# First stage of a graph-attention and expert kernel: four buffers a hand-over, longer lags, and one half of a quarter's encoding ahead of the softmax's exponential

## Chip, cores, metric

One core of one Trainium2 chip. The metric is the device time of one execution in microseconds (us), the median of several.

## What is computed

```python
x = x + elu(attention @ Wh)        # a graph-attention layer on layernorm(x)
x = x + expert_ffn(layernorm(x))   # then a feed-forward layer, one expert a row
# x: 8192 x 256 f32, adj: 8192 x 8192 int32, ones at a rate of 0.000488
def gnn(h, adj, W, a):
    Wh = h @ W                                     # 256 x 256
    e = (Wh @ a1)[:, None] + (Wh @ a2)[None, :]
    e = where(e > 0, e, 0.2 * e)
    e = where(adj > 0, e, -9e15)
    return elu(softmax(e, axis=1) @ Wh)
def ffn(x, router_w, router_b, W1, b1, W2, b2):    # 32 experts, hidden size 64
    idx = argmax(x @ router_w.T + router_b)
    return relu(relu(x @ W1[idx] + b1[idx]) @ W2[idx] + b2[idx])
```

## The kernel before

The 8192 rows are 64 strips of 128. The work has three stages, and each engine runs an order written out by hand, with semaphores between the engines.

**First stage** (8 groups of 8 strips; functions `group` and `prepare`). Each strip s goes through a line of engines: VectorE normalises it (`normalise`, L985, into `xn`), GpSimd adds it to a running sum (`row_sum`, L583), TensorE transposes it (L1485), ScalarE copies the transpose out of PSUM (L709, into `xT`), TensorE multiplies it with the weights (L1494, into `psW`), VectorE copies the 258 columns to the table rows (`table_rows`, L993). `xn`, `xT`, the PSUM tiles of the transposes and `psW` have two buffers each. TensorE's order is T(s), W(s-1), where T is the pair of transposes and W the product; VectorE's is N(s), C(s-2), where N is the normalising and C the copy. Both empty the line at a group's end. In the second half of a group VectorE also takes the statistics of the next group (L967, two strips a step) and at its end the variances (L973, L975); GpSimd then takes the power -1/2 of all eight (`inverse_stds`, L569), without which the next group's N(0) can't start. After the group's last C, GpSimd writes the eight table rows to HBM (L593). One buffer of the means (`mv`) and of the inverse deviations (`rs`) serves all groups.

Beside this, each group handles one half strip of `adj`: SyncE loads it (L427, 2 MB, three buffers), ScalarE turns the int32 entries into two sets of fp8 signs (`signs`: L717 the even bytes, L719 the odd ones, a quarter strip at a time, two quarters a group, after strips 2 and 6), TensorE folds them at the group's end (`fold`, L1512 and L1514, into `psF`), and VectorE takes the largest words (`search`, L891), right after the next group's N(0). After every second group VectorE decodes the columns found (L897 to L957), spread over the even groups.

At the end of the stage the mean row goes through TensorE and VectorE and is written to HBM (L598); when all writes have landed, GpSimd starts the first gathers (L611).

**Second stage**: 64 rounds u, one strip each, four strips ahead in `adj`. GpSimd gathers the table rows of the columns found (L611) and scatters finished rows to their expert's region (L633); VectorE computes scores and softmax, decodes, places; ScalarE encodes four quarters of `adj` a round (`signs`, eight instructions of L717 and L719) and takes the softmax's exponential (`softmax_exp`, L749), which waits for the row maximum of VectorE (`nmx`, L1106). SyncE issues the load of a half strip when ScalarE has finished the half that lay in its buffer.

**Third stage**: the experts' blocks, unchanged.

Of the kernel before, what the change touches and what calls it, by code (L numbers as in the profile page):

```python
# [5 lines left out]
P = 128  # L6
D = 256
DH = D // P
# [12 lines left out]
THIRDS = 3  # L21
FOLD = 8
PAIRS = FOLD // 2
GROUP = 8
# [12 lines left out]
def gat_moe(nc, x, adj, gW, ga, rw, rb, W1, b1, W2, b2, out, table, region):  # L37
# [23 lines left out]
    with ctx:  # L61
# [106 lines left out]
        diag = sb("diag", [P, 8, P])  # L168
# [64 lines left out]
        psXn = [psT, psO[0]]  # L233
# [286 lines left out]
        def _(pool):  # L520
# [44 lines left out]
            def inverse_stds(g):  # L565

                pool.wait_ge(v_var, g + 1)
                pool.nop(nofuse=True)
                pool.tensor_tensor(rs[:, :], ve[:, :], minus_half[:, :], ALU.pow).then_inc(pl_rs, 1)  # L569
# [7 lines left out]
            def row_sum(s, r):  # L577
# [5 lines left out]
                pool.tensor_tensor(xn_sum[:, :], xn_sum[:, :], xn[r % 2][:, :], ALU.add).then_inc(pl_sum, 1)  # L583

            def group(g, par, i, behind, ahead):
                for r in range(GROUP):
                    row_sum(g * GROUP + r, r)
                if ahead:
                    inverse_stds(g + 1)
# [101 lines left out]
        def _(act):  # L691
# [12 lines left out]
            def transposes(s, r):  # L704

                act.wait_ge(pe_xT, s + 1 + 2)
                act.wait_ge(pe_wh, s + 1)
                act.nop(nofuse=True)
                act.activation(xT[r % 2][:, :, :].rearrange("p h n -> p (h n)"), psXn[r % 2][:, 0:D], ACT.Copy).then_inc(a_xT, 1)  # L709

            def signs(t, par, q, strip):
# [5 lines left out]
                act.activation(sign_of[par][q][0], raw_of[b][q % 2][0], ACT.Identity, bias=minus_tiny[:, 0:1], scale=TINY,  # L717
                               saturate=False)
                act.activation(sign_of[par][q][1], raw_of[b][q % 2][1], ACT.Sign, bias=minus_half[:, 0:1],  # L719
                               saturate=False).then_inc(a_sg, 1)  # L720
# [45 lines left out]
            def step(u, par, do, strip):  # L766
# [8 lines left out]
                if do.ahead:  # L775
                    signs(u + LAG + 1, 1 - par, 1, strip)
# [954 lines left out]
```

## Time and profile before

| | us |
|---|---|
| median of 3 runs (1185.07 to 1197.87) | 1185.52 |
| profiled execution | 1188.4 |
| its span, first to last instruction | 1186.6 |
| first stage, first N to last C | 24.2 to 147.7 |
| second stage, first to last exponential | 176.3 to 1006.8 |

The profiled execution has 1.8 us outside its span, and is 2.9 us above the median.

### The profile page before, as it was taken

How to read it: one execution, taken by the hardware profiler on the slowest of the kernel's cores; microseconds unless marked ns; L12 is line 12 of the kernel's file. 1: busy time of each engine (PE TensorE's matmuls, PEld its weight loads, DVE VectorE, ACT ScalarE, POOL GpSimd, SP SyncE). 2: the span in 40 equal slices, each digit the busy share in tenths (PEclk: the TensorE clock that was granted, in tenths of full speed). 3: DMA queues.
4: the chain of work that ended last, by engine and by line, in shares of the span. 5: the costliest groups of instructions: out<-in, count | busy, mean ns of one | idle time of the engine just before them, and what ended most of it. 6: DMA issues, size and time to landing. Idle time of an engine off the chain costs nothing.

```text
span 1186.6 us, 25008 instructions
## 1 busy us (share of the span) xinstructions
PE 900.9 (76%) x4388; PEld 560.6 (47%) x4389; DVE 894.5 (75%) x4327; ACT 795.4 (67%) x1339; POOL 656.9 (55%) x700
## 2 busy tenths in 40 slices
PE   2777728788878888688887878878888875558995
PEld 1545515444444444354454444445445444446774
DVE  5788727688888878788888878878888876555563
ACT  0444549688887878688788877878878831136663
POOL 3555545556656655555565556655566556326664
PEclk9999959899999989899999999989999986679998
DMA  6677788899999999899999989998999995035651
GB/s 227 219 270 266 295 335 345 318 376 377 376 371 368 362 349 365 330 341 381 363 381 349 368 323 371 366 361 336 374 381 383 341 251 129 29 105 162 173 170 60
DMA packets 84715, 357.33 MB, mean 301 GB/s; under 512 B 26006, under 2 KB 52591, under 8 KB 68289
## 3 DMA queue, kind: packets, MB, share of 16 engines
q1 hardware_dynamic: 56226, 296.78, 67.7%
q0 software_dynamic: 27712, 60.06, 14.7%
q8 instruction: 12, 0.20, 0.1%
q14 instruction: 29, 0.24, 0.1%
q10 hardware_dynamic: 736, 0.05, 0.0%
HBM read 343.67 MB, written 32.05 MB: 317 GB/s over the span
## 4 chain that ended last, share of the span: by engine, by line
DVE 29%; DMA 23%; issue 22%; PE 13%; POOL 7%; DVEq 2%; ACT 2%; POOLq 0%; ACTq 0%
DMA regions<-x,posu 13%; DMA G_all<-wh_table,idx 7%; POOL G_all L611 4%; PE psO L1704 2%; DVE top_word L891 2%; PE psW L1494 2%; PE psO L1577 2%; POOL out_x L673 2%; DVE xn L1158 1%; DVE begun L1058 1%; DVE lidx L1173 1%; PE psO L1503 1%; DVE oh L1181 1%; DVE xn L985 1%; DVE el L1132 1%
## 5 line engine op out<-in xcount | busy, mean ns | idle before, releaser
L611 POOL DMA_INDIRECT G_all<-wh_table,idx x384 | 398.7, 1038 | 136.4 <-issue 128.7
L717 ACT ACTIVATE sg<-raw_all,minus_tiny 128x1024 fp8e4<-128x1024 int32 x256 | 311.8, 1218 | 0.1
L719 ACT ACTIVATE sg<-raw_all,minus_half 128x1024 fp8e4<-128x1024 int32 x256 | 311.1, 1215 | 0.0
L1503 PE MATMUL psO<-word_no,share 128*128 128x512 bf16 x885 | 244.0, 411 | 0.0
L633 POOL DMA_INDIRECT regions<-x,posu x64 | 67.4, 1053 | 213.9 <-DVE idx L1050 115.7
L1577 PE MATMUL psO<-G_all,diag 128*128 128x256 f32 x640 | 163.2, 405 | 22.9 <-DVE diag L1115 22.9
L1577 PEld LDWEIGHTS psO<-G_all,diag 128*128 128x128 f32 x640 | 124.3, 201 | 64.9 <-issue 48.4
L1512 PE MATMUL psF<-sg,fold_w 128*128 128x512 bf16 x512 | 136.0, 389 | 7.3 <-DVE top_word L891 2.7
L1503 PEld LDWEIGHTS psO<-word_no,share 128*128 128x128 bf16 x885 | 93.6, 111 | 92.9 <-issue 26.8
L749 ACT ACTIVATE pr<-ee,nmx 128x16 f32<-128x16 f32 x64 | 19.7, 307 | 146.3 <-DVE nmx L1106 146.3
L673 POOL DMA_INDIRECT out_x<-raw_all,tok x81 | 78.9, 974 | 56.6 <-issue 29.9
L891 DVE MAX8 top_word<-psF 128x8 f32<-128x256 f32 x256 | 103.0, 425 | 6.7 <-PE psF L1514 0.5
L1494 PE MATMUL psW<-w_aug,xT 128*128 128x258 f32 x256 | 69.5, 395 | 13.8 <-ACT xT L709 13.8
L583 POOL TENSOR_TENSOR xn_sum<-xn_sum,xn 128x256 f32<-128x256 f32 x64 | 47.5, 742 | 40.7 <-DVE xn L985 39.8
L1512 PEld LDWEIGHTS psF<-sg,fold_w 128*128 128x128 bf16 x512 | 47.1, 108 | 43.8 <-issue 13.4
L1704 PE MATMUL psO<-x_sb,hT 128*128 x162 | 56.0, 428 | 8.9 <-ACT hT L825 3.7
L1563 PE MATMUL psW<-slot_s,to_row 128*128 128x11 f32 x128 | 22.3, 248 | 49.3 <-DVE slot_s L1086 49.1
L627 POOL TENSOR_TENSOR x<-ve,minus_half 128x1 f32<-128x1 f32 x64 | 36.8, 576 | 35.6 <-DVE x L1154 34.7
L1563 PEld LDWEIGHTS psW<-slot_s,to_row 128*128 128x128 f32 x128 | 22.8, 204 | 69.8 <-issue 68.7
L1494 PEld LDWEIGHTS psW<-w_aug,xT 128*128 128x128 f32 x256 | 44.8, 195 | 22.7 <-issue 18.9
L817 ACT ACTIVATE w_b<-x_sb 128x129 f32 x84 | 26.3, 313 | 43.0 <-ACT hT L825 30.2
L1086 DVE TENSOR_SCALAR slot_s<-slot_col,G_all 128x11 f32<-128x11 f32 x64 | 16.6, 260 | 47.9 <-DMA G_all<-wh_table,idx 46.9
(217 smaller groups left out, 1837.5 us busy)
## 6 DMA issues: line engine op xcount, KB each, us to landing
raw_all<-in_adj SPq DMA_DIRECT2D x128, 2048.0 KB, 10.0
raw_all<-regions SPq DMA_DIRECT2D x84, 130.0 KB, 2.2
wh_table<-G_all POOLq DMA_DIRECT2D x8, 1040.0 KB, 10.0
x_sb<-in_x SPq DMA_DIRECT2D x8, 1024.0 KB, 5.7
G_all<-wh_table,idx POOLq DMA_INDIRECT x384, 6.1
regions<-pad_row SPq DMA_DIRECT2D x32, 130.0 KB
x_sb<-in_L_ffn_W SPq DMA_DIRECT2D x4, 512.0 KB
x_sb<-in_L_ffn_W SPq DMA_DIRECT2D x8, 256.0 KB
```

The costliest lines, as they stand in the source:

```text
L583: pool.tensor_tensor(xn_sum[:, :], xn_sum[:, :], xn[r % 2][:, :], ALU.add).then_inc(pl_sum, 1)
L611: pool.indirect_dma_start(out=G[par][:, k, :], out_offset=None, in_=table[:, :], in_offset=bass.IndirectOffsetOnAxis(ap=idx[par][:, k:k + ...
L633: pool.indirect_dma_start(out=region[:, :], out_offset=bass.IndirectOffsetOnAxis(ap=posu[par][:, 0:1], axis=0), in_=x1[par][:, :], in_offs ...
L673: pool.indirect_dma_start(out=out[:, :], out_offset=bass.IndirectOffsetOnAxis(ap=tok[r % STORES][:, 0:1], axis=0), in_=yb[r % STORES][:, : ...
L717: act.activation(sign_of[par][q][0], raw_of[b][q % 2][0], ACT.Identity, bias=minus_tiny[:, 0:1], scale=TINY, saturate=False)
L719: act.activation(sign_of[par][q][1], raw_of[b][q % 2][1], ACT.Sign, bias=minus_half[:, 0:1], saturate=False).then_inc(a_sg, 1)
L891: v.max(top_word[:, q, :], psF[q // 2][:, q % 2 * WORDS:(q % 2 + 1) * WORDS]).then_inc(v_top, 1)
L1494: mm = pe.matmul(psW[r % 2][:, 0:D + 2], xT[r % 2][:, h, :], w_aug[:, h, :], start=(h == 0), stop=(h == DH - 1))
L1503: pe.matmul(psO[par][:, :], share[:, :], word_no[:, 0:2, :].rearrange("p q w -> p (q w)"), start=True, stop=True)
L1512: pe.matmul(words, fold_w[:, j, :], sg[par][:, 2 * h:2 * h + 2, j * WORDS:(j + 1) * WORDS], start=(j == 0), stop=False)
L1577: pe.matmul(psO[par][:, 0:D], diag[:, k, :], G[par][:, k, 0:D], start=(k == 0), stop=False)
L1704: pe.matmul(psO[r % 2][:, 0:D], hT[r % 2][:, :], w2_sb[:, bass.ds(e, 1), :].rearrange("p o n -> p (o n)"), start=True, stop=True).then_inc ...
```

## The change

In the first stage `xn` and `xT` get four buffers (the two new ones lie in `diag`, which is free until the second stage), the transposes' PSUM tiles three, `mv` and `rs` two. TensorE's order becomes T(s), W(s-2) and VectorE's N(s), C(s-3), across the groups' borders; only the last group empties the line. The next group's statistics move to strips 2 to 5, the variances behind strip 5, the power behind the sixth row sum. A group's table write moves behind the third row sum of the next group. ScalarE encodes one instruction after every second strip rather than two after every fourth. SyncE issues a group's x and `adj` loads when two strips of the group two before are normalised, six strips earlier. The fold stays at the group's end in TensorE's order, then behind T(7) and W(5). In the second stage the even bytes of the third quarter are encoded ahead of the exponential; the odd ones stay behind `elu_exp`.

```diff
+COPY_LAG = 3
...
-        mv = sb("mv", [P, GROUP, 2])
+        mv = [sb(f"mv{i}", [P, GROUP, 2]) for i in range(2)]
-        rs = sb("rs", [P, GROUP])
-        xn = [sb(f"xn{i}", [P, D]) for i in range(2)]
-        xT = [sb(f"xT{i}", [P, DH, P]) for i in range(2)]
+        rs = [sb(f"rs{i}", [P, GROUP]) for i in range(2)]
+        diag = sb("diag", [P, 8, P])
+        xn = [sb(f"xn{i}", [P, D]) for i in range(2)] + [diag[:, 2 * i:2 * i + 2, :].rearrange("p h n -> p (h n)") for i in range(2)]
+        xT = [sb(f"xT{i}", [P, DH, P]) for i in range(2)] + [diag[:, 4 + 2 * i:6 + 2 * i, :] for i in range(2)]
...
-        psXn = [psT, psO[0]]
+        psXn = [psT, psO[0], psO[1]]
...
@@ load_group (SyncE)
-                sp.wait_ge(v_xn, g * GROUP + GROUP)
+                sp.wait_ge(v_xn, g * GROUP + 2)
@@ group (GpSimd)
+            def group(g, par, i, behind, ahead):
+                for r in range(GROUP):
+                    row_sum(g * GROUP + r, r)
+                    if behind and r == COPY_LAG - 1:
+                        write_rows(g - 1, 1 - par)
+                    if ahead and r == 5:
+                        inverse_stds(g + 1)
             groups(pool, group)
+            write_rows(NG - 1, (NG - 1) % 2)
@@ transposes, group (ScalarE)
-                act.wait_ge(pe_wh, s + 1)
+                if s >= 4:
+                    act.wait_ge(pe_wh, s - 1)
...
-                    if r % 4 == 2:
-                        signs(i, i % 2, 2 * par + r // 4, divmod(i, THIRDS))
+                    if r % 2 == 0:
+                        signs(i, i % 2, 2 * par + r // 4, divmod(i, THIRDS), range(r // 2 % 2, r // 2 % 2 + 1))
@@ step (ScalarE)
                 if do.ahead:
                     signs(u + LAG + 1, 1 - par, 1, strip)
+                    signs(u + LAG + 1, 1 - par, 2, strip, range(1))
                 if do.attend:
                     softmax_exp(u)
                 if do.post:
                     elu_exp(u - 1)
                 if do.ahead:
-                    signs(u + LAG + 1, 1 - par, 2, strip)
+                    signs(u + LAG + 1, 1 - par, 2, strip, range(1, 2))
                     signs(u + LAG + 1, 1 - par, 3, strip)
@@ normalise, prepare (VectorE)
-                v.wait_ge(pe_xT, s + 1)
-                if s >= 2:
-                    v.wait_ge(pl_sum, s - 1)
+                if s >= 4:
+                    v.wait_ge(pe_xT, s - 1)
+                    v.wait_ge(pl_sum, s - 3)
...
-                    if r >= 2:
-                        table_rows(g, par, i, r - 2)
-                    if ahead and r >= GROUP // 2:
+                    if g * GROUP + r >= COPY_LAG:
+                        table_rows(g * GROUP + r - COPY_LAG)
+                    if ahead and 2 <= r < 6:
                         for k in range(2):
-                            group_stats(g + 1, 1 - par, next_i, (r - GROUP // 2) * 2 + k)
-                if ahead:
-                    group_variances(g + 1)
-                table_rows(g, par, i, GROUP - 2)
-                table_rows(g, par, i, GROUP - 1)
+                            group_stats(g + 1, 1 - par, next_i, (r - 2) * 2 + k)
+                    if ahead and r == 5:
+                        group_variances(g + 1)
@@ transposes, group (TensorE)
-                pe.wait_ge(a_xT, s + 1)
+                if s >= 3:
+                    pe.wait_ge(a_xT, s)
...
                     transposes(g * GROUP + r, r)
-                    if r:
-                        table_rows(g * GROUP + r - 1, r - 1)
-                table_rows(g * GROUP + GROUP - 1, GROUP - 1)
+                    if g * GROUP + r >= 2:
+                        table_rows(g * GROUP + r - 2, r)
                 fold(i, i % 2, par)
```

## Rows read from the trace of the kernel before

**Rows 1.** The page, busy tenths in 40 slices of the span.
```profile
DVE  5788727688888878788888878878888876555563
DMA  6677788899999999899999989998999995035651
```
**Rows 2.** Windows of the first stage: the stage, an even group, an odd group.
```profile
24.20:147.30 123.10, 92.39 (x421) 61.48 (x422) 92.82 (x317) 60.56 (x104) 66.20 (x79) 1.00 0.71 252
86.98:102.80 15.82, 11.47 (x54) 7.42 (x53) 13.96 (x54) 7.27 (x12) 8.52 (x10) 1.00 0.76 267
102.80:117.74 14.94, 11.26 (x54) 7.49 (x53) 11.07 (x39) 7.21 (x12) 8.56 (x10) 1.00 0.80 279
```
**Rows 3.** Timeline (start, duration, engine), end of an even group, start of the next.
```profile
96.93 0.39 DVE L985 TENSOR_SCALAR xn<-x_sb,mv,rs 128x256 f32<-128x256 f32 x1
...
97.47 0.41 PE L1485 MATMUL psT<-ident,xn 128*128 128x128 f32 x2 [0.94 <-DVE xn L985]
...
97.71 1.04 PE L1494 MATMUL psW<-w_aug,xT 128*128 128x258 f32 x4
...
100.73 0.42 DVE L993 COPY G_all<-psW 128x258 f32<-128x258 f32 x1
100.97 1.65 POOL L569 TENSOR_TENSOR rs<-ve,minus_half 128x8 f32<-128x8 f32 x1 [1.44 <-DVE ve L975]
...
101.03 1.11 PE L1494 MATMUL psW<-w_aug,xT 128*128 128x258 f32 x4 [0.98 <-ACT xT L709]
...
101.98 1.02 PE L1512 MATMUL psF<-sg,fold_w 128*128 128x512 bf16 x4
...
102.84 0.38 PE L1514 MATMUL psF<-word_no,share 128*128 128x512 bf16 x1
...
103.36 0.76 DVE L891 MAX8 top_word<-psF 128x8 f32<-128x256 f32 x2 [0.15 <-PE psF L1514]
```
**Rows 4.** Timeline, two VectorE instructions that meet a row sum, first stage.
```profile
91.65 0.82 DVE L932 SCALAR_TENSOR_TENSOR key<-bits,code 128x128 f32<-128x128 int32 x1
...
105.12 0.90 DVE L985 TENSOR_SCALAR xn<-x_sb,mv,rs 128x256 f32<-128x256 f32 x1 [0.69 <-POOL xn_sum L583]
```
**Rows 5.** Timeline of the first group: two copies and the variances.
```profile
31.64 0.43 DVE L993 COPY G_all<-psW 128x258 f32<-128x258 f32 x1 [1.40 <-PE psW L1494]
...
32.89 0.43 DVE L993 COPY G_all<-psW 128x258 f32<-128x258 f32 x1 [0.50 <-PE psW L1494]
...
38.93 0.17 DVE L975 TENSOR_SCALAR ve<-mv 128x8 f32<-128x8 f32 x1
```
**Rows 6.** Timeline, the last V, the stage's last copy, the mean's write, the first gather.
```profile
131.51 0.42 DVE L993 COPY G_all<-psW 128x258 f32<-128x258 f32 x1
...
147.26 0.43 DVE L993 COPY G_all<-psW 128x258 f32<-128x258 f32 x1 [1.86 <-PE psW L1494]
...
151.07 0.55 POOL L598 DMA_DIRECT2D wh_table<-mean_sb  x1 [1.91 <-DVE mean_sb L1044]
...
163.03 1.14 POOL L611 DMA_INDIRECT G_all<-wh_table,idx  x1 [11.41 <-issue]
```
**Rows 7.** Waits from 300 to 900 us: total, times, longest.
```profile
ACT pr L749 <- DVE nmx L1106: 91.2, 44, 6.5
...
DVE slot_s L1086 <- DMA G_all<-wh_table,idx: 18.6, 8, 4.6
DVE x L1140 <- DMA regions<-x,posu: 17.4, 20, 1.6
```
**Rows 8.** Timeline of ScalarE, the exponential of one round.
```profile
604.44 0.31 ACT L749 ACTIVATE pr<-ee,nmx 128x16 f32<-128x16 f32 x1 [1.98 <-DVE nmx L1106]
```
**Rows 9.** One line of the source, L427: the adjacency loads.
```profile
DMA to landing us min/median/max: 7.3/10.0/11.8
```
**Rows 10.** Timeline, the power and a VectorE instruction at once, second stage.
```profile
597.01 0.59 POOL L627 TENSOR_TENSOR x<-ve,minus_half 128x1 f32<-128x1 f32 x1
597.02 0.28 DVE L1058 TENSOR_SCALAR begun<-slot_no,tail_row 128x128 f32<-128x128 f32 x1
```

More of the change, by code:

```diff
@@ L568, in inverse_stds @@
                 pool.nop(nofuse=True)
[L569 removed]
+                pool.tensor_tensor(rs[g % 2][:, :], ve[:, :], minus_half[:, :], ALU.pow).then_inc(pl_rs, 1)
             inverse_stds(0)
@@ L582, in row_sum, with write_rows @@
                 pool.nop(nofuse=True)
[L583 to L587, printed above, removed]
-                if ahead:
-                    inverse_stds(g + 1)
+                pool.tensor_tensor(xn_sum[:, :], xn_sum[:, :], xn[r % 4][:, :], ALU.add).then_inc(pl_sum, 1)
+            def write_rows(g, par):
                 pool.wait_ge(v_wh, g * GROUP + GROUP + 2)
@@ L706, in transposes, with signs @@
                 act.wait_ge(pe_xT, s + 1 + 2)
-                act.wait_ge(pe_wh, s + 1)
+                if s >= 4:
+                    act.wait_ge(pe_wh, s - 1)
                 act.nop(nofuse=True)
-                act.activation(xT[r % 2][:, :, :].rearrange("p h n -> p (h n)"), psXn[r % 2][:, 0:D], ACT.Copy).then_inc(a_xT, 1)
-            def signs(t, par, q, strip):
+                act.activation(xT[s % 4][:, :, :].rearrange("p h n -> p (h n)"), psXn[s % 3][:, 0:D], ACT.Copy).then_inc(a_xT, 1)
+            def signs(t, par, q, strip, bytes=range(2)):
                 b, count = half_place(strip, q // 2)
@@ L716, in signs @@
                 act.nop(nofuse=True)
[L717 to L720, printed above, removed]
+                if 0 in bytes:
+                    act.activation(sign_of[par][q][0], raw_of[b][q % 2][0], ACT.Identity, bias=minus_tiny[:, 0:1], scale=TINY,
+                                   saturate=False)
+                if 1 in bytes:
+                    act.activation(sign_of[par][q][1], raw_of[b][q % 2][1], ACT.Sign, bias=minus_half[:, 0:1],
+                                   saturate=False).then_inc(a_sg, 1)
             def group(g, par, i, behind, ahead):
@@ L972, in group_variances @@
                 for r in range(GROUP):
-                    v.bn_aggr(mv[:, r, :], st[:, r, :]).then_inc(v_st, 1)
+                    v.bn_aggr(mv[g % 2][:, r, :], st[:, r, :]).then_inc(v_st, 1)
                 v.wait_ge(v_st, g * 2 * GROUP + 2 * GROUP)
-                v.tensor_scalar(ve[:, :], mv[:, :, 1], EPS, None, ALU.add).then_inc(v_var, 1)
+                v.tensor_scalar(ve[:, :], mv[g % 2][:, :, 1], EPS, None, ALU.add).then_inc(v_var, 1)
             def normalise(g, par, r):
@@ L981, in normalise, with table_rows @@
                     v.wait_ge(pl_rs, g + 1)
-                v.wait_ge(pe_xT, s + 1)
-                if s >= 2:
-                    v.wait_ge(pl_sum, s - 1)
-                v.tensor_scalar(xn[r % 2][:, :], x_rows(s), mv[:, r, 0:1], rs[:, r:r + 1],
+                if s >= 4:
+                    v.wait_ge(pe_xT, s - 1)
+                    v.wait_ge(pl_sum, s - 3)
+                v.tensor_scalar(xn[s % 4][:, :], x_rows(s), mv[par][:, r, 0:1], rs[par][:, r:r + 1],
                                 ALU.subtract, ALU.mult).then_inc(v_xn, 1)
-            def table_rows(g, par, i, r):
-                v.wait_ge(pe_wh, g * GROUP + r + 1 + 2)
+            def table_rows(s):
+                g, r = divmod(s, GROUP)
+                i, par = divmod(g, 2)
+                v.wait_ge(pe_wh, s + 1 + 2)
                 if r == 0:
@@ L1039, in _ @@
             groups(v, prepare)
+            for s in range(NS - COPY_LAG, NS):
+                table_rows(s)
             v.wait_ge(pe_sum, 1)
@@ L1481, in transposes @@
                 pe.wait_ge(v_xn, s + 1 + 2 * GROUP)
-                pe.wait_ge(a_xT, s + 1)
+                if s >= 3:
+                    pe.wait_ge(a_xT, s)
                 pe.nop(nofuse=True)
                 for h in range(DH):
-                    mm = pe.transpose(psXn[r % 2][:, h * P:(h + 1) * P], xn[r % 2][:, h * P:(h + 1) * P], ident[:, :])
+                    mm = pe.transpose(psXn[s % 3][:, h * P:(h + 1) * P], xn[s % 4][:, h * P:(h + 1) * P], ident[:, :])
                 mm.then_inc(pe_xT, 1)
@@ L1493, in table_rows @@
                 for h in range(DH):
-                    mm = pe.matmul(psW[r % 2][:, 0:D + 2], xT[r % 2][:, h, :], w_aug[:, h, :],
+                    mm = pe.matmul(psW[s % 2][:, 0:D + 2], xT[s % 4][:, h, :], w_aug[:, h, :],
                                    start=(h == 0), stop=(h == DH - 1))
@@ L1524, in _ @@
             groups(pe, group)
+            for s in range(NS - 2, NS):
+                table_rows(s, s)
             pe.wait_ge(pl_sum, NS)
```

9 lines of the change are left out of this document (4 added, 5 removed).

## The prediction

> **What bounds the kernel now.** I read the page's slices first [rows 1]: up to slice 5 (148 us) both VectorE and the DMA engines have gaps, then the DMA engines stand at 9 tenths nearly everywhere and VectorE at 7 or 8. So the two halves of the change fall on stages with different limits. The windows of the first stage [rows 2] say that no engine fills it: in 123.1 us VectorE is busy 92.8, TensorE 92.4, GpSimd 66.2, ScalarE 60.6. An even group, which also decodes, takes 15.82 us with VectorE busy 13.96; an odd one 14.94 with 11.07. VectorE's idle time is thus 1.86 and 3.87 us a group. It is the engine nearest to its bound, and in even groups there is little left.
>
> The timeline at a group's end [rows 3] shows where that idle time is. Let V be the moment after the variances, 100.73. The power runs from 100.97 to 102.62; TensorE's last product starts at 101.03, the fold at 101.98, its last matmul at 102.84, and the search starts at 103.36, V+2.63. Between V and there VectorE does two copies, two small ones and N(0), about 1.4 us, and idles 1.2.
>
> **First stage, the group's end.** The change runs the power under N(6), C(3), N(7), C(4), and so seems to take the wait away. But the fold stays behind T(7) and W(5) in TensorE's order, and N(6) and N(7) now come after the variances. I walk it with the steps of [rows 3]:
> - N(6) starts at V. A transpose starts 0.54 after its N (96.93 to 97.47), the product 0.24 later (97.71): T(6) at V+0.54, W(4) at V+0.78.
> - What follows a product starts 0.95 after it (101.03 to 101.98): T(7) at V+1.7, W(5) at V+1.95, the fold at V+2.9.
> - The fold's last matmul comes 0.86 after its first (101.98 to 102.84), the search 0.52 after that (to 103.36): V+4.3.
>
> Within these 4.3 us VectorE has N(6), C(3), N(7), C(4), N(0): with 0.40 and 0.43 each, less some overlap, 1.7 us. It idles 2.6 us, not 1.2. The power ends at V+1.9 and is hidden; the fold is what is late next.
>
> **First stage, the rest of a group.** Elsewhere an odd group idles 3.87 - 1.2 = 2.7 us now. The longer lags take most of it: W(s-2) finds its xT finished, and N(s) needs no sum of two strips ago. What stays is C(7) behind W(7) behind T(1) behind the late N(1), some 0.9 us by the same steps (N(1) follows the search; 0.54 + 0.24 + 1.1 for T and W, less N(2) in between). An N that meets a row sum under way takes 0.90 rather than 0.40 [rows 4]; an odd group has two such, 0.9 us together. With the table write in mid-group, not ahead of the sums, GpSimd isn't behind there, and these 0.9 us go. Odd group: 11.07 - 0.9 + 2.6 + 0.8 = 13.6, against 14.94: 1.3 to 1.4 us better. Even group: it idles 1.86 - 1.2 = 0.66 elsewhere, which goes, and two N give back 0.6; the `key` instruction that runs into a row sum, 0.82 [rows 4], stays, since it follows N as before. 13.96 - 0.6 + 2.6 = 16.0, against 15.82: 0.2 worse. Odd groups 1, 3, 5: -4.1; even groups 2, 4, 6: +0.5.
>
> **First group.** Its statistics move into waits for the slow first products. Now C(1) starts at 31.64 and C(2) at 32.89 [rows 5], and the variances at 38.93. After: C(1) at 31.6, a pair of statistics and N(5) beside W(2), C(2) at about 33.0, two more statistics (0.7), the variances (0.75): V at 34.5 rather than 39.0. This is -4.4.
>
> **Last group.** No statistics, and the line empties in the order T(7), W(5), fold, W(6), W(7). With 1.1 us a product the last copy starts some 17.3 us after the last V; now it is 15.8 (131.51 to 147.26, [rows 6]): +1.5. The mean's write at 151.07 waits for TensorE's last sum, which now stands behind the fold, and after behind W(7): only +0.5 to +0.8 there. The first gather, 163.03, waits for that write's landing and the last table write's, which come within 1 us of each other: +0.7.
>
> **The other edits** of this stage I cost at nothing. The loads issued six strips earlier use DMA engines that idle between 24 and 37 us [rows 1]; SyncE's queue keeps its order and its wait for ScalarE. The table write queues behind the third row sum and waits for C(7) at most 1 us; behind it stand row sums 3 and on, four strips ahead of their reader. If one write landed 4 us late, C(0) of the group after the next would wait for it. Encoding in single instructions halves the time that an xT can stand behind them.
>
> Sum of the first stage: -4.4 - 4.1 + 0.5 + 0.7 = -7.3 us. The second stage starts at a landing, not at a clock, so all of it is passed on.
>
> **Second stage.** ScalarE waits for `nmx` 91.2 us in 44 rounds, 2.07 a round [rows 7], at [rows 8] 1.98. One encoding instruction (1.2 us, 1.1 from start to start) fits in; and of the waits that I saw hardly one is under 1.1 (the shortest 1.04), so the exponential is not late. It finishes its quarter 1.1 us earlier, and so does the release of the buffer. But ScalarE then waits for the next keys; VectorE sees nothing. What VectorE waits for here is DMA: 18.6 us for gathers in 8 rounds and 17.4 for scatters in 20 [rows 7]. The moved instruction needs the half strip's second half 1.1 us earlier after a release that is 13 us old, and the loads land in at most 11.8 [rows 9]: a bound of nothing above, one late load below. Every second load is issued 1.1 us earlier, and they lie more evenly (by the ends of ScalarE's second and fourth quarters 5.7 and 7.5 us apart now, 6.8 and 6.4 after), which may spare or add DMA waits: no row shows this, so I bound it by the row of the scatters, half of 17.4 either way, and take 0, as the engines are at 9 tenths already.
>
> **Sum.** The profiled execution 1188.4 (span 1186.6 plus 1.8) less 7.3 is 1181.1; it stands 2.9 above the median, so the forecast on the median's scale is 1185.5 - 7.3 = 1178.2.
>
> **A rule against it.** A row sum in progress stretches N to 0.90 [rows 4]. A power does not: `begun`, a tensor_scalar of 128x128 that starts 0.01 us after it, takes 0.28 [rows 10], less than an undisturbed N of twice the columns. The Trainium skill (SBUF — State Buffer, SBUF: two separate sides) says that VectorE in a two-port mode and GpSimd take a shared pair of ports by an exclusive lock for the whole instruction, and the loser blocks; by that, N(7) would wait for the power's end. The row of the sums agrees with it, the row of the power doesn't.
>
> **Rivals.**
> - *The power of eight columns blocks N(7) after all* (it is 1.65 us long in the first stage, 0.59 in [rows 10]). N(7) would end at V+2.05, T(7) start at V+2.2, and the search at V+4.75: 0.5 more in seven groups, 3.5. Then 1185.5 - 3.8 = 1182. Against it: [rows 10]. 0.13.
> - *The fold is not late*, and VectorE runs at its own work: odd groups 10.2 + 1.2 = 11.4, even ones 13.4 + 0.5 = 13.9, so 3 x 3.5 + 3 x 1.9 + 4.4 - 0.7 = 19.9: 1166; or the fold is late, and the evener loads spare half the scatter waits: 1178 - 9 = 1169. For it: the idle time is there; against it, the order of TensorE's queue. 0.22 together.
> - *Slower: earlier releases bunch the loads onto the gathers.* The place is VectorE's wait for the gather of the slots (`slot_s`, now 18.6 us in 8 rounds, the longest 4.6, [rows 7]). With three more of the longest it is -7.3 + 13.8 = +6.5, 1192; it decides from two on, and passes 1% at five. For it: DMA at 9 tenths; against: two loads a round remain, with evener distances. 0.10.
> - *The gain is not passed on*: the adjacency stream, not the start, sets the second stage's end, and the stage takes back what it started early: 1185. For it: DMA at 9 tenths; against: ScalarE's releases, not bytes, pace the loads. 0.12.
> - The forecast itself: 0.43, its own range 1174 to 1182.
>
> **How the numbers follow.** A measurement here tells about 1% (12 us) from no change. The range reaches from the second rival's 1166, a little further for both its parts together, to the slow rival's near side: 1164 to 1190. Faster by over 1%, below 1173.7: all of the second rival and a fifth of the forecast, 0.31. Slower by over 1%, above 1197.4: the far half of the slow rival, 0.05. The rest is 0.64.
>
> **What would show it.** In the profile after: V of the first group at 34.5; odd groups 13.6 and even ones 16.0 from search to search; VectorE idle ahead of the search on the fold (now 0.15, after about 1.4); no wait of N for a row sum in odd groups; the last C at about 140; first gather near 156; exponentials after a wait of 0.3 to 0.9 and the same distances of 12.4 and 13.4. I am wrong if the odd and even groups lose more than 1.5 us each, if the power stretches N(7), or if the second stage's length of 830 us between first and last exponential changes by more than 8.

## The result, and the profile after

The changed kernel takes 1209.93 us (median of 4 runs, 1205.33 to 1211.92) against 1185.39 for the kernel before on the same chip: ratio 1.0233, 95% interval 1.0175 to 1.0291. It is slower by about 25 us where I had forecast 7 us faster. Its profiled execution took 1210.87 us, with a span of 1209.1.

**Where the time went.** Two moments split the profiled executions: the last C of the first stage and the softmax's exponentials (first and last).

| us | before | after |
|---|---|---|
| start of the last C | 147.3 | 146.9 |
| first exponential | 176.3 | 177.5 |
| first to last exponential | 841.2 | 862.4 |

(The 830 us that the prediction gives for the last row, and the 1006.8 in the table of the profile before, leave out the 64th exponential, 10.7 us after the 63rd.) So the first stage gained nothing, and the second lost 21 us. The page's slices, to be read beside [rows 1]:

```profile
DVE  5877627888878888888887888878887876555563
DMA  7668769999999999999998999989998996135552
```

They show nearly nothing: 2.5% of a stage spread over 63 rounds doesn't reach a tenth of a slice. The waits from 300 to 900 us do show it (engine, line, releaser: us in total, times, longest), against [rows 7]:

```profile
DVE slot_s L1099 <- DMA G_all<-wh_table,idx: 49.4, 22, 5.7
...
DVE x L1153 <- DMA regions<-x,posu: 0.6, 2, 0.3
```

VectorE's wait for a gather went from 18.6 us in 8 rounds to 49.4 in 22, which is every second round of this window. The wait for a scatter went from 17.4 to 0.6, presumably because a scatter has landed by the time that a late round asks for it; no run isolates that. Net, 14 us in 600, hence some 20 over the stage.

**What a late round looks like.** Timeline after: the last gather of a round, the load issued ahead of it on SyncE's queue (SPq), and the reader of the gathers.

```profile
602.12 0.33 SPq L428 DMA_DIRECT2D raw_all<-in_adj  x1
...
602.25 1.01 POOL L617 DMA_INDIRECT G_all<-wh_table,idx  x1 [0.30 <-DVE x L1167]
...
609.35 0.23 DVE L1099 TENSOR_SCALAR slot_s<-slot_col,G_all 128x11 f32<-128x11 f32 x1 [1.88 <-DMA G_all<-wh_table,idx]
```

The same three in a round of the kernel before:

```profile
595.98 1.01 POOL L611 DMA_INDIRECT G_all<-wh_table,idx  x1 [0.30 <-issue]
596.96 0.33 SPq L427 DMA_DIRECT2D raw_all<-in_adj  x1
...
601.53 0.30 DVE L1086 TENSOR_SCALAR slot_s<-slot_col,G_all 128x11 f32<-128x11 f32 x1
```

Before, the load of 2 MB goes out 0.98 us behind the last gather, and the reader comes 5.55 us after the gather without a wait. After, the load is 0.13 us ahead of it, and the gather's data is there only 7.1 us after its issue, 1.88 later than VectorE wanted it. Between 420 and 620 us after, all seven late rounds have the load 0.11 to 0.14 us ahead and a wait of 1.81 to 2.24; in the rounds between them the load is 0.9 to 2.6 behind, and there is no wait. From 300 to 900 us it is 21 of 21 rounds with the load ahead that wait, and none of 18 with it 0.9 us or more behind. ScalarE's exponentials show both kinds of round:

```profile
585.06 0.31 ACT L758 ACTIVATE pr<-ee,nmx 128x16 f32<-128x16 f32 x1 [2.66 <-DVE nmx L1119]
...
597.31 0.31 ACT L758 ACTIVATE pr<-ee,nmx 128x16 f32<-128x16 f32 x1 [0.26 <-DVE nmx L1119]
...
612.24 0.31 ACT L758 ACTIVATE pr<-ee,nmx 128x16 f32<-128x16 f32 x1 [2.72 <-DVE nmx L1119]
```

They lie 12.25 and 14.93 us apart, where in the kernel before 13.39 and 12.38 us lie ahead of and behind the one of [rows 8]: 1.4 us more for this pair. Over the whole stage it is 0.7 a pair (21 us over 63 distances), since the kernel before has more rounds of 16 to 19 us, six against four, among its shorter ones. ScalarE's wait for `nmx`, 1.98 in [rows 8], is 0.26 in one kind of round and 2.7 in the other, and its total even fell (91.2 in [rows 7], 71.4 after): a wait that falls on one engine is no gain when another paces the round.

**The first stage.** Timeline after, end of the first group; to be read beside [rows 3]:

```profile
34.02 0.17 DVE L985 TENSOR_SCALAR ve<-mv 128x8 f32<-128x8 f32 x1
34.10 0.41 DVE L995 TENSOR_SCALAR diag<-x_sb,mv,rs 128x256 f32<-128x256 f32 x1
34.33 1.71 POOL L570 TENSOR_TENSOR rs<-ve,minus_half 128x8 f32<-128x8 f32 x1 [1.19 <-DVE ve L985]
...
34.77 0.40 DVE L995 TENSOR_SCALAR diag<-x_sb,mv,rs 128x256 f32<-128x256 f32 x1
...
34.91 1.04 PE L1508 MATMUL psW<-w_aug,xT 128*128 128x258 f32 x4
...
35.78 0.38 PE L1499 MATMUL psO<-ident,diag 128*128 128x128 f32 x2
...
36.88 1.02 PE L1526 MATMUL psF<-sg,fold_w 128*128 128x512 bf16 x4
...
38.22 0.77 DVE L901 MAX8 top_word<-psF 128x8 f32<-128x256 f32 x2 [1.32 <-remote]
```

(`diag` is where the new `xn` buffers lie, and "remote" stands for a releaser that this view couldn't name; in a later profile of the same kernel it is TensorE's fold.) V is 34.10, forecast 34.5; W(4) at V+0.81, T(7) at V+1.68, the fold at V+2.78, the search at V+4.12 after a wait of 1.32: forecast V+0.78, 1.7, 2.9 and 4.3. N(7) ran in 0.40 with the power in progress. But two odd groups went another way. Windows of the stage, of odd group 3, of an even group and of odd group 5 (the column after GpSimd's is TensorE's granted clock, then DMA share and GB/s), beside [rows 2]:

```profile
23.79:146.90 123.11, 92.78 (x419) 64.89 (x427) 91.33 (x317) 63.73 (x106) 65.69 (x79) 0.96 0.71 256
64.56:81.30 16.74, 13.81 (x52) 9.22 (x53) 10.67 (x38) 7.53 (x12) 8.41 (x10) 0.80 0.54 202
81.30:97.70 16.40, 10.73 (x52) 7.43 (x53) 13.71 (x52) 7.42 (x12) 8.52 (x10) 1.00 0.86 309
97.70:113.14 15.44, 12.39 (x52) 8.68 (x53) 10.80 (x38) 7.52 (x12) 8.41 (x10) 0.89 0.61 218
```

The granted clock was 1.00 throughout in [rows 2]. Here it is 0.80 and 0.89 over two groups, and the matmuls at one place show what that means:

```profile
65.13 0.66 PE L1499 MATMUL psO<-ident,diag 128*128 128x128 f32 x2 [1.91 <-DVE diag L995]
...
65.58 1.93 PE L1508 MATMUL psW<-w_aug,xT 128*128 128x258 f32 x4
...
69.44 1.90 PE L1526 MATMUL psF<-sg,fold_w 128*128 128x512 bf16 x4
```

1.93 where the same four took 1.04 in the first group: half the clock, so the 1.2 GHz level, at the end of 1.91 us in which TensorE had stood idle. And the stage's end, beside [rows 6]:

```profile
146.88 0.43 DVE L1005 COPY G_all<-psW 128x258 f32<-128x258 f32 x1 [0.45 <-PE psW L1508]
...
149.88 0.55 POOL L604 DMA_DIRECT2D wh_table<-mean_sb  x1 [1.11 <-DVE mean_sb L1057]
...
165.51 1.14 POOL L617 DMA_INDIRECT G_all<-wh_table,idx  x1 [15.08 <-issue]
```

The mean's write goes out 1.2 us earlier than before, and the first gather comes 2.5 us later: from write to gather 15.6 us instead of 12.0. From 147.30 to 165.50, the window from the last C to that gather, the DMA engines stand at a share of 1.01 and 418 GB/s.

### The profile page after: what moved, and what is told of

It is laid out like the page before. It is cut to its first block, busy times and chain, and to the rows that moved or that the text cites. A ratio compares the mean times of both kernels' runs of the same rounds, so it can differ in the third digit from the quotient of the medians.

```text
span 1209.1 us, 25012 instructions
## 1 busy us (share of the span) xinstructions
PE 897.3 (74%) x4321; PEld 574.0 (47%) x4389; DVE 894.1 (74%) x4327; ACT 801.2 (66%) x1339; POOL 656.2 (54%) x700
## 3 DMA queue, kind: packets, MB, share of 16 engines
q0 software_dynamic: 27712, 60.06, 14.9%
## 4 chain that ended last, share of the span: by engine, by line
DVE 29%; DMA 22%; issue 20%; PE 10%; POOL 4%; DVEq 3%; ACT 1%; POOLq 0%; ACTq 0%; another core or an unknown queue 0%
DMA G_all<-wh_table,idx 18%; PE psO L1719 3%; DVE top_word L901 3%; POOL G_all L617 2%; DMA regions<-x,posu 2%; DVE el L1145 2%; PE psO L1592 2%; DMA wh_table<-mean_sb 1%; DVE code L935 1%; POOL out_x L679 1%; DVE rest_word L912 1%; DVE sc L1113 1%; DVE xn L1171 1%; PE psL L1708 1%; PE psW L1708 1%
## 5 line engine op out<-in xcount | busy, mean ns | idle before, releaser
L1517 PE MATMUL psO<-word_no,share 128*128 128x512 bf16 x827 | 228.4, 407 | 3.0
L639 POOL DMA_INDIRECT regions<-x,posu x64 | 67.5, 1054 | 210.2 <-DVE idx L1063 121.4
L1526 PE MATMUL psF<-sg,fold_w 128*128 128x512 bf16 x512 | 147.8, 416 | 8.3 <-DVE top_word L901 2.9
L1592 PEld LDWEIGHTS psO<-G_all,diag 128*128 128x128 f32 x640 | 127.6, 204 | 54.0 <-issue 35.4
L1099 DVE TENSOR_SCALAR slot_s<-slot_col,G_all 128x11 f32<-128x11 f32 x64 | 15.6, 244 | 90.2 <-DMA G_all<-wh_table,idx 90.2
L742 ACT ACTIVATE hh<-psO,rden 128x256 f32<-128x256 f32 x64 | 30.4, 475 | 76.3 <-PE psO L1594 75.1
L633 POOL TENSOR_TENSOR x<-ve,minus_half 128x1 f32<-128x1 f32 x64 | 36.8, 575 | 60.2 <-DVE x L1167 59.4
L827 ACT ACTIVATE w_b<-x_sb 128x129 f32 x84 | 26.2, 312 | 43.2 <-ACT hT L835 30.9
L1584 PEld LDWEIGHTS psW<-pr,to_slot 128*128 128x128 f32 x128 | 28.1, 250 | 55.1 <-issue 53.5
L1128 DVE TENSOR_TENSOR diag<-ident,pr 128x640 f32<-128x640 f32 x64 | 51.5, 805 | 0.0
```

The lines of the kernel that those rows point to most:

```text
L639: pool.indirect_dma_start(out=region[:, :], out_offset=bass.IndirectOffsetOnAxis(ap=posu[par][:, 0:1], axis=0), in_=x1[par][:, :], in_offs ...
L1128: v.tensor_tensor(diag[:, 0:KD, :], ident[:, :].unsqueeze(1).to_broadcast([P, KD, P]), pr[:, 0:KD].unsqueeze(2).to_broadcast([P, KD, P]), ...
L1517: pe.matmul(psO[par][:, :], share[:, :], word_no[:, 0:2, :].rearrange("p q w -> p (q w)"), start=True, stop=True)
L1526: pe.matmul(words, fold_w[:, j, :], sg[par][:, 2 * h:2 * h + 2, j * WORDS:(j + 1) * WORDS], start=(j == 0), stop=False)
L1592: pe.matmul(psO[par][:, 0:D], diag[:, k, :], G[par][:, k, 0:D], start=(k == 0), stop=False)
```

## The experiments

The runs were made on several chips. On the two that served the first eight, the kernel before takes 1238.65 and 1236.24 us; on the two that served the last eight it takes 1187.74 and 1188.02, close to the result's 1185.39. The profiled runs had a mean granted clock of 0.887 to 0.914 on the first two and 0.915 to 0.936 on the others. Ratios are each to the kernel before on the same chip, and absolute times are only compared inside a group.

### One part at a time

The first-stage part alone (the diff without the two lines in the second stage's `step`):

```diff
-                    signs(u + LAG + 1, 1 - par, 2, strip, range(1))
...
-                    signs(u + LAG + 1, 1 - par, 2, strip, range(1, 2))
+                    signs(u + LAG + 1, 1 - par, 2, strip)
```

> The first stage's part alone, the encoding order of before. Theory of the release: the 21 us lost between first and last exponential come from the encoding ahead of the exponential, so the second stage is as long as before (830 us) and the whole within 3 us of before (1183 to 1189): the first stage gives nothing by itself (last table copy at 146.9 against 147.3, first gather 2.5 us later). Rival, the start's phase: the first stage leaves buffers and queues in another state, and the rounds of 15 us come with it, 1203 to 1210.

Measured: ratio 1.0093 (1.0065 to 1.0120). The first exponential came at 173.5 us, but the exponentials then spread over 874 us, with only 3.5 us of waits for gathers. That is neither of the two outcomes that I had named.

The encoding edit alone (those two lines on the kernel before):

> The encoding edit alone on the kernel before. Theory of the release: 1204 to 1210, rounds of 12.2 and 15 us in turn, the slots' gather waited for some 50 us between 300 and 900 us. Rival, the start's phase: 1184 to 1188.

Measured: 1.0138 (1.0097 to 1.0179), waits of `slot_s` for gathers 29.2 us in 24 rounds, the last C at 146.9.

The ratio's interval overlaps the lower end of what I had expected, and the waits are well short of the 50 us. One of these rounds:

```profile
516.93 1.01 POOL L611 DMA_INDIRECT G_all<-wh_table,idx  x1 [0.30 <-issue]
517.28 0.21 SPq L427 DMA_DIRECT2D raw_all<-in_adj  x1
...
524.19 0.23 DVE L1089 TENSOR_SCALAR slot_s<-slot_col,G_all 128x11 f32<-128x11 f32 x1 [1.09 <-DMA G_all<-wh_table,idx]
```

Here the load is 0.35 us *behind* the last gather, and VectorE still waits 1.09. Between 300 and 900 us 16 rounds of this run have the load 0.32 to 0.66 behind, and all 16 wait (19.8 us together); of the six with the load about 0.1 ahead four wait, 2.4 us together; of the 17 with it 1.25 or more behind none does. So the load needn't be ahead of the gather to make it late: on this chip it was enough that it went out while GpSimd was still at work on the gather's instruction, which takes 1.0 us.

Both parts alone are slower on this chip. The second points straight at the gathers; the first doesn't.

### The loads released later

The theory by now: a load issued ahead of the round's last gather, or close behind it, makes the gather land late. To test it without taking a wait away, the load is made to wait for something that comes after the gather's issue: ScalarE's copy of the attention sum (`hh`), which raises the semaphore `a_h`. (A later expectation calls this instruction the exponential; it is the copy.)

```diff
                 if do.ahead:
+                    if not isinstance(u, int) or u >= 2:
+                        sp.wait_ge(a_h, u + 1)
+                        sp.nop(nofuse=True)
                     load_strip(u + LAG + 1, strip)
```

On the whole change:

> The changed kernel, but SyncE issues each strip's first load only when ScalarE has also copied the attention sum that follows its last quarter, which comes after the last gather's issue. Theory of the release: the load's descriptors no longer go ahead of the last gather's; the wait for the slots' gather falls from 49 to under 20 us, and the whole to 1185 to 1192. Rival, the order on ScalarE itself (the exponential behind one more instruction, the attention sum waiting for TensorE): no change, 1205 to 1212.

Measured: 1.0010 (0.9981 to 1.0040), one wait for a gather, 1.8 us. On the kernel before:

> The kernel before with the same later load alone (some 0.5 us later). Theory of the release: 1180 to 1188, since the load already goes out after the last gather; it may take some of the waits for gathers away. Rival: loads 0.5 us later cost 0.5 us in each of 56 rounds if the adjacency stream is what bounds, 1205 or more.

Measured: 0.9980 (0.9953 to 1.0008). The late release by itself is worth nothing beyond its interval, and with it the change no longer costs anything on this chip, where the encoding edit alone cost 1.4%. The rival, that the order of ScalarE's instructions is the cost, would have kept the change slow: that order is the same here.

### Where the buffers lie

The change also moves SBUF places: `diag` is declared earlier. The kernel before with the new places, and the first-stage part with the old ones, beside one more run of each of the two kernels:

> The kernel before once more, for its profile on the same chip as the three that follow. On the chip of the four experiments the second stage's rounds were nearer to 14 us than to 13.4 in every kernel; I expect the same lengths here as on one of the two chips, and no wait for the slots' gather that is longer than some 20 us between 300 and 900 us.

> The changed kernel once more, on the same chip as its parts. The first stage alone cost 0.9% and the encoding alone 1.4%: if the two costs add, 1.023 again.

> The first stage's part alone, with diag and the second mv and rs placed in SBUF as in the kernel before. Theory of the layout: the 0.9% of the first stage's part comes from moved addresses in the second stage, ratio 0.995 to 1.000 (first gather 2 us earlier, the rest as before). Rival, the schedule: the ratio stays at 1.009.

> The kernel before with the SBUF places of the changed one and nothing else. Theory of the layout: 1.007 to 1.011. Rival, the schedule: 0.998 to 1.002.

Measured: the kernel before took 1240.8 us in its single run, with 10.2 us of waits for gathers in 5 rounds; the whole change stood at 1.0146 (1.0089 to 1.0203), with 26.2 in 24. So the costs of the two parts don't add, though I had written 1.023 for the case that they do: on such a chip the whole change costs what the encoding edit costs alone. The first-stage part with the old places came to 1.0062 (1.0035 to 1.0089), so it is slower without the new places too; the kernel before with the new ones to 1.0006 (0.9969 to 1.0044). The places are out as the cause of the cost.

### Each part with the late release, and the search one strip later

> Only the encoding edit, and from the third load on the load of the adjacency waits for the exponential of the round before it. In the two comparisons made so far the encoding edit alone cost 1.4% with 29 us of waits of slot_s for the gathers. Theory A (the load is issued ahead of the round's last gather and the gather lands late): the waits for the gathers fall under 5 us, and the ratio is 0.997 to 1.002. Rival B (the order of the two encodings and the exponential on ScalarE is itself the cost, and the gather wait only a place where it shows): the ratio stays 1.010 to 1.018, with another wait grown by about as much (slot_s, the product pr or hh).

> Only the first-stage part, with the same late release of the loads. Alone the part came out at 1.009 and 1.006 although its first exponential is 2 to 3 us earlier. Theory A (its cost too is when the loads are issued in the rounds of the second stage): ratio 0.995 to 1.001. Rival B (its cost lies elsewhere, for instance in a clock of TensorE that is granted lower after a busier first stage): ratio 1.006 to 1.009, and the sum over the exponentials stays 8 to 15 us above that of the kernel before on this chip.

The third and fourth kernels of this group address the search's wait for the fold. On VectorE the search and every decode step move one strip later, and the last group's two last products go ahead of its fold:

```diff
-                    if par == 1 and r == 0:
+                    if par == 1 and r == 1:
...
-                    if behind and par == 0 and r == 0:
+                    if behind and par == 0 and r == 1:
...
+                if not ahead:
+                    for s in range(NS - 2, NS):
+                        table_rows(s, s)
                 fold(i, i % 2, par)
```

> The first-stage part with the late release, and the search and decode on VectorE one strip later (the first at r = 1 in the group after the fold), with the last group's last two table matmuls ahead of its fold. No encoding edit. In the trace of the changed kernel the search waits about 1.4 us for the fold in five groups of seven and 3.4 in one. Theory A (that wait is on the path of the first stage): the waits for the fold go under 0.3 us each, the last C comes 7 to 10 us earlier than in the first-stage part alone, so at 134 to 137 instead of 143.8, and the ratio is 0.990 to 0.996. Rival B (the wait overlaps TensorE's own lateness, which is next): the last C within 2 us of 143.8, ratio 0.996 to 1.003.

> As the run with the shifted search, and the encoding edit as well: the whole change, with the late release and the shifted search. With the late release alone the whole change stood at 1.001. Theory A: the encoding edit is worth nothing once the loads are late, so this comes within 0.003 of the kernel with the shifted search and without the edit (0.990 to 0.997). Rival B (the edit gains something when the loads no longer cost): 0.003 to 0.008 below that kernel. The waits of slot_s for the gathers are under 5 us under both.

Measured:

| | ratio (95% interval) | last C | first exponential | first to last |
|---|---|---|---|---|
| encoding edit, late release | 0.9965 (0.9930 to 1.0000) | 148.0 | 177.2 | 838.4 |
| first-stage part, late release | 0.9905 (0.9867 to 0.9943) | 145.8 | 175.7 | 831.4 |
| the same, search later | 0.9871 (0.9820 to 0.9922) | 137.0 | 166.4 | 832.7 |
| the same and the encoding edit | 0.9838 (0.9794 to 0.9882) | 136.8 | 165.4 | 834.8 |

The encoding edit with the late release, last gather of a round, load, reader:

```profile
608.93 1.00 POOL L614 DMA_INDIRECT G_all<-wh_table,idx  x1 [0.30 <-issue]
...
610.37 0.33 SPq L427 DMA_DIRECT2D raw_all<-in_adj  x1
...
613.93 0.23 DVE L1092 TENSOR_SCALAR slot_s<-slot_col,G_all 128x11 f32<-128x11 f32 x1
```

The load is back behind the gather, by 1.44, and the reader comes 5.0 us after it with no wait. The order of the instructions on ScalarE is the same as in the encoding edit alone, so that order isn't the cost. Over 300 to 900 us the waits of `slot_s` are 8.3 us in 5 rounds: more than the 5 that I had set, though far from 29; 6.1 of them fall in the two rounds whose load is only 0.12 and 0.17 behind the gather. The first-stage part gained more (0.9905) than my theory's range of 0.995 to 1.001 allowed, and with the later search (0.9871) again more than 0.990 to 0.996. The two kernels with the later search have 13.5 and 14.9 us of waits for gathers, where I had named under 5 for the last. With the search one strip later VectorE waits for the fold 0.40 or 0.43 us in each of the seven groups, a little over the 0.3 that I had named, and the last C comes at 137.0, inside the forecast 134 to 137. Timeline of this kernel, the variances at both ends of an odd group and the search between them:

```profile
63.79 0.17 DVE L987 TENSOR_SCALAR ve<-mv 128x8 f32<-128x8 f32 x1
...
68.03 0.76 DVE L903 MAX8 top_word<-psF 128x8 f32<-128x256 f32 x2 [0.43 <-remote]
...
76.76 0.17 DVE L987 TENSOR_SCALAR ve<-mv 128x8 f32<-128x8 f32 x1
```

This odd group takes 12.97 us from variances to variances. The last kernel is the fastest of the study, 1.6% below the kernel before and 3.8% below the change as it stood (0.9838 against 1.0222 where the kernel before takes the same). The later search by itself moves the first exponential by 9 us (175.7 to 166.4), part of which is the clock: in the profile of the second row two groups took 1.7 and some 1.5 us more at the lower level. It moves the ratio by 0.3%, which the intervals don't separate from the 0.8% that 9 us would be. The encoding edit is worth 0.3% in it, which is inside the intervals: not shown to be a gain.

### All parts on one chip

What was left open were ratios taken on different chips. So the whole change, its two parts and the late release alone went onto one chip on which the kernel before takes 1188.02:

> The whole change once more, beside its parts on one chip. Theory A (the loads' release is the cost): 1.012 to 1.025, with 25 to 50 us of waits of slot_s for the gathers between 300 and 900 us.

> The first-stage part alone. With the late release it stood at 0.9905. Theory A (its cost on the earlier chips was the release of the loads): 1.002 to 1.010 here too. Rival B (that cost was the chip, and the part gains by itself): 0.988 to 0.996, with under 6 us of waits of slot_s for the gathers.

> The encoding edit alone. With the late release it stood at 0.9965. Theory A: 1.010 to 1.020 with over 20 us of waits of slot_s for the gathers, so the whole of the change's cost comes in with this edit. Rival B (the two parts share the cost): 1.003 to 1.008.

> The kernel before with the late release alone. If the late release is worth something only where the loads were early: 0.997 to 1.001, and the gain of the first-stage part with it (0.9905) is that part's own. If the late release is a gain by itself on a fast chip: 0.990 to 0.994, and most of the 0.9905 was its.

Measured. The left column and the 0.9982 are of this chip; the 0.9965 and 0.9905 are of the chip before it (kernel before 1187.74), and the 1.0010 is of the first one:

| | loads as they are | loads released late |
|---|---|---|
| kernel before | 1 | 0.9982 (0.9944 to 1.0021) |
| encoding edit alone | 1.0248 (1.0168 to 1.0329) | 0.9965 (0.9930 to 1.0000) |
| first-stage part alone | 1.0052 (1.0010 to 1.0094) | 0.9905 (0.9867 to 0.9943) |
| whole change | 1.0222 (1.0152 to 1.0292) | 1.0010 (0.9981 to 1.0040; the encoding edit alone is 1.0138 on that chip) |

The whole of the cost comes in with the encoding edit, and all of it leaves with the late release. The second half of this compares ratios across chips, since no kernel with the encoding edit ran with and without the late release on one chip; what stands on one chip is 1.0138 for the edit alone against 1.0010 for the whole change with the late release. The encoding edit alone cost more than the 1.010 to 1.020 that I had written, the other three came as the theory said. The whole change had 50.2 us of waits for gathers in 22 rounds here, as in the result. The encoding edit alone, waits of 300 to 900 us, then one of its late rounds:

```profile
DVE slot_s L1089 <- DMA G_all<-wh_table,idx: 53.1, 22, 5.4
```

```profile
604.01 0.33 SPq L427 DMA_DIRECT2D raw_all<-in_adj  x1
604.11 1.01 POOL L611 DMA_INDIRECT G_all<-wh_table,idx  x1 [0.30 <-issue]
...
611.58 0.23 DVE L1089 TENSOR_SCALAR slot_s<-slot_col,G_all 128x11 f32<-128x11 f32 x1 [2.25 <-DMA G_all<-wh_table,idx]
```

The same order, load 0.10 ahead of the gather, and the same two microseconds, with the first stage of the kernel before. Between 300 and 900 us this run and the whole change on this chip each have 21 rounds with the load 0.09 to 0.17 ahead, and all 42 wait, in the middle 1.9 and 2.0 us; of their 33 rounds with it 1.5 us or more behind none does.

The first-stage part alone shows the first stage nearly undisturbed: TensorE's clock held where the whole change lost it, and fell only from 121.4 to 124.8 us, in an even group whose length (16.40) shows nothing of it. Windows of the stage, of an even and of an odd group, and the timeline of the variances and searches:

```profile
24.00:147.00 123.00, 92.38 (x434) 64.54 (x434) 93.46 (x325) 67.21 (x109) 67.11 (x82) 0.99 0.74 268
49.05:65.59 16.54, 10.91 (x53) 7.50 (x53) 13.60 (x52) 7.51 (x12) 8.50 (x10) 1.00 0.84 304
65.59:79.34 13.75, 10.88 (x53) 7.50 (x53) 10.81 (x37) 7.43 (x12) 8.39 (x10) 1.00 0.67 243
```

```profile
65.59 0.17 DVE L984 TENSOR_SCALAR ve<-mv 128x8 f32<-128x8 f32 x1
...
69.82 0.76 DVE L900 MAX8 top_word<-psF 128x8 f32<-128x256 f32 x2 [1.37 <-PE psF L1527]
...
79.34 0.17 DVE L984 TENSOR_SCALAR ve<-mv 128x8 f32<-128x8 f32 x1
```

Its odd groups take 13.93, 13.75 and 13.76 us and its even ones 16.54, 16.41 and 16.40, against 15.0 and 15.8 to 16.0 for the kernel before with late loads on this chip. The last C comes at 143.3 and the first exponential at 173.5, 3.9 and 3.2 us earlier than there.

In the same odd group, two N that still meet work of GpSimd, a row sum and the table write that the change moved there:

```profile
71.40 0.73 POOL L584 TENSOR_TENSOR xn_sum<-xn_sum,xn 128x256 f32<-128x256 f32 x1 [1.39 <-DVE xn L994]
71.48 0.79 DVE L994 TENSOR_SCALAR diag<-x_sb,mv,rs 128x256 f32<-128x256 f32 x1
...
73.69 0.92 POOL L590 DMA_DIRECT2D wh_table<-G_all  x1 [0.52 <-DVE G_all L1004]
73.98 0.73 DVE L994 TENSOR_SCALAR diag<-x_sb,mv,rs 128x256 f32<-128x256 f32 x1
```

## Why the prediction was wrong

**The step that failed** is the last of "Second stage": "Every second load is issued 1.1 us earlier, and they lie more evenly [...] no row shows this, so I bound it by the row of the scatters, half of 17.4 either way, and take 0". It measured +21 us between first and last exponential, over twice the bound. A row did show it, and I hadn't looked at it: the distance from a round's last gather to the load behind it. In 40 of the 45 rounds of the kernel before between 300 and 900 us it is 0.86 to 1.39 us (19 rounds up to 1.02, 21 from 1.32), and the edit moves the load 1.1 us forward. So the margin was smaller than the shift in about every second round. The waits of [rows 7] point there too: 11.0 of the 18.6 us fall in five of those 19 rounds with the small margin, 3.9 in the one round whose load is ahead of its gather. I had measured the loads against each other (5.7 and 7.5 us, to become 6.8 and 6.4), and their evenness says nothing of the one neighbour on another queue that they were about to pass.

**The slow rival** named the right mechanism and place, loads bunched onto the gathers and the wait of `slot_s`, and gave it 0.10. Its price was wrong in form: "three more of the longest", 13.8 us, where it was about 2 us in every second round, 14 more such waits in the window of 600 us (22 for 8). A mechanism that sits in the loop's order comes in every round that has the order, not a few times. And what I held against it, the evener distances, was no argument.

**The exponential** isn't what costs the time, as forecast, since with the late release the same order of ScalarE's instructions costs nothing. But its wait, forecast as 0.3 to 0.9 us, is 0.17 to 0.27 in 15 of the 21 short rounds between 300 and 900 us and 0.05 or less in the other six. There ScalarE has no slack left, which was luck rather than the margin that I had claimed.

**First stage, the walk at the group's end** held to 0.2 us: the search at V+4.12 for V+4.3, the wait for the fold 1.32 for 1.4. The fold is what is late next; the rival that it is not, is out, and moving the search one strip later took the wait to 0.4: from the first group's variances to the last's it is 84.4 us (35.41 to 119.77), and 90.8 in the first-stage part alone (35.12 to 125.91), 1.1 a group.

**The power** doesn't block N(7): 0.40 us for N(7) at 34.77 with the power running from 34.33 to 36.04. The trace didn't agree with the Trainium skill here (SBUF — State Buffer, SBUF: two separate sides), by which the loser of the port pair would have blocked until 36.04. That N takes part in such a contest at all is shown only by its 0.79 us beside a row sum. The row that I held against that rival, [rows 10], was the right guide.

**The sizes of the first stage**, by the first-stage part alone beside the kernel before with late loads, on one chip:

| | forecast | measured |
|---|---|---|
| first group (38.77 to 35.12) | -4.4 | -3.7 |
| odd groups, three | -4.1 | -3.5 |
| even groups, three | +0.5 | +1.7 |
| last group, to its last C | +1.5 | +1.6 |
| last C | -6.5 | -3.9 |

The even groups were mis-sized: 16.4 to 16.5 us for 16.0. The odd ones took 13.8 to 13.9 for 13.6. One term was wrong in both: the time that N would get back by no longer meeting a row sum, 0.9 us in an odd group and 0.6 in an even one. In the odd group from 65.59 three N still take 0.56, 0.79 and 0.73, together 0.88 over their 0.40, as much as before; an even group gets back 0.15 to 0.25. VectorE is therefore busy 10.81 us in this odd group, where the sum had 10.2, and 13.60 in the even one shown for 13.4. That the odd groups came within 0.2 to 0.3 all the same is luck: VectorE idles 2.9 us there and not 3.4. Then two terms that weren't in the sum. In the profiled execution of the whole change two odd groups ran partly at the lower clock, 16.74 and 15.44 for 13.75: +4.7 us. And from the mean's write to the first gather it took 3.7 us longer than before; for the pair on one chip it is 15.1 us (146.33 to 161.45) against 12.6 (150.98 to 163.61). I had taken that stretch as unchanged, and what lengthens it wasn't tested. So of the -6.5 at the last C -0.4 was left, and the forecast -7.3 at the first exponential became +1.3; in the pair on one chip it was -3.2.

**The rival that the gain isn't passed on** is out: with late loads and the search shifted, the first exponential comes at 166.4 against 176.6 for the kernel before with late loads (on another chip of nearly the same speed), and from there to the last it takes 832.7 us against 842.9: the stage doesn't take the early start back.

**What stays open.** The first-stage part alone costs 0.5% with the loads as they are, in spite of an earlier start, and gains 0.95% with the loads late, where the late release alone gives 0.2%, inside its interval. The profile of the first fits half of it (19.4 us of waits for gathers in 13 rounds, against 8.1 in 7 with the late release and 840.9 against 831.4 us between exponentials), but its own span, 1182.8, isn't slower than that of before. On the chip where the kernel before takes 1238.65 the same part cost 0.9% with hardly a wait for gathers. That the load's phase to the gathers matters there too is argued from the late release, not shown by a row. Nor was a load issued later by other means, or the gather alone delayed, tried.

## What to carry to other kernels

When an edit moves a transfer's issue, look up what is issued next to it on the other queues, and compare the shift with that distance: here a shift of 1.1 us over a margin of 0.86 to 1.02 put a 2 MB load ahead of the gather that VectorE waits for, in every second round. With the DMA engines busy at 9 tenths the earlier release wasn't free; a wait that holds the bulk transfer behind the urgent one cost nothing (0.998) and took 2.8% back (1.0248 to 0.9965, on two chips of nearly the same speed). And a mechanism that lies in a loop's order is priced by the number of rounds, not by the longest wait seen so far.

## What I had not expected of the hardware

- **A bulk load 0.1 us ahead of a gather delays its landing by about 2 us**, though both have their own queue: in three profiles (the changed kernel twice, the encoding edit alone) all 63 rounds with the load 0.09 to 0.17 us ahead make VectorE wait, and the gather's data is used 6.6 to 8.1 us after its issue in 57 of them, later in six. Being ahead isn't needed: on the chip of the second experiment 16 of 16 rounds with the load 0.32 to 0.66 behind waited too. A load about 1 us behind isn't wholly safe: 7 of those 40 rounds of the kernel before waited, though 5.0 to 5.6 us were enough in most. The Trainium skill (DMA: Bandwidth & Descriptors, Issuing engines are not separate DMA queues) says that DMAs started by the sync and the GpSimd engine run on the same 16 DMA engines and interleave. That fits the direction; that one microsecond of order decides so much, no sentence there says.
- **TensorE's clock fell inside a stage where it had been 1.00**, to 0.50 (1.2 GHz), from 64.4 to 71.2 us and again from 98.5 to 101.9, both times in or right behind a wait of TensorE of 1.9 us for N(6). The pause alone doesn't decide it: with the same wait of 1.90 the clock didn't fall at that place in the first-stage part alone, and in the kernel with the later search it fell from 59.4 to 62.8 without a wait of TensorE over 1.7. The fall cost 3 us in one group (16.74 for 13.75), and nothing where TensorE had slack. What brings it on isn't settled: the profiles of the changed kernel on two chips lost the clock at 65 us in both, then at 98 in one and at 127 in the other.
